# Recurrence stage: the second normalisation and the feed-forward part move one slot back

## The reference

```python
xa = _ln(x, ln1_w, ln1_b)
sx = shifted(xa) - xa
xxx = tanh((xa + sx * maa_x) @ maa_w1).reshape(b, l, 5, DM) ... @ maa_w2
xk, xw, xv, xr, xg = xa + sx * (maa_stack + xxx)
w = exp(-exp(time_decay + tanh(xw @ td_w1) @ td_w2))
r, k, v, g = xr @ Wr.T, xk @ Wk.T, xv @ Wv.T, silu(xg @ Wg.T)
# over the tokens, per head: out = r (u k v + s);  s = k v + w s
og = group_norm(out) * gn_w + gn_b
x1 = x + og * g @ Wo.T
xc = _ln(x1, ln2_w, ln2_b)
sx2 = shifted(xc) - xc
rr = sigmoid((xc + sx2 * ffn_maa_r) @ Wfr.T)
kk = square(relu((xc + sx2 * ffn_maa_k) @ Wfk.T))
return x1 + rr * (kk @ Wfv.T)
```

## Time and profile before

| | us |
|---|---|
| median of 3 runs | 2136.84 (2136.43 to 2137.71) |
| profiled execution | 2138.01, its span 2136.3 |
| TensorE busy | 1944.2 (91% of the span) |
| VectorE busy | 1261.8 (59%) |
| ScalarE busy | 1085.0 (51%) |
| GpSimd busy | 516.4 (24%) |

### The profile page before, as it was taken

One profiled execution on the slowest core, in us unless ns is written; L12 is line 12 of the kernel. 1 busy time (PEld: TensorE's weight loads), 2 busy tenths in 40 slices (PEclk: granted clock), 3 DMA queues, 4 the chain that ended last, 5 costly groups with the idle time before them and its releaser, 6 DMA issues. The chain is left out here.

```text
span 2136.3 us, 40585 instructions
## 1 busy us (share of the span) xinstructions
PE 1944.2 (91%) x15496; PEld 1692.5 (79%) x15496; DVE 1261.8 (59%) x2546; ACT 1085.0 (51%) x2920; POOL 516.4 (24%) x346
## 2 busy tenths in 40 slices
PE   6999996999999999999899999999988986898974
PEld 4677764997999999999699999999978984566653
DVE  6888886235645555555465555555552364888883
ACT  3787877545443344443453344334446543566653
POOL 3555453544200000000240000000005514324220
PEclk9999998999999999999999999999998997899986
DMA  5000001300000000002200000000020000000000
GB/s 188 2 2 2 2 2 42 117 1 6 6 6 5 0 5 5 5 5 90 74 6 1 5 5 5 5 0 5 29 89 1 1 1 1 1 11 6 6 11 10
DMA packets 29534, 40.72 MB, mean 19 GB/s; under 512 B 1923, under 2 KB 21477, under 8 KB 29157
## 3 DMA queue, kind: packets, MB, share of 16 engines
q1 hardware_dynamic: 29412, 39.06, 5.4%
HBM read 32.76 MB, written 2.10 MB: 16 GB/s over the span
## 5 line engine op out<-in xcount | busy, mean ns | idle before, releaser
L761 DVE TENSOR_TENSOR w_head_lo<-banks,w_head_hi 128x512 fp32r<-128x512 f32 x128 | 88.1, 691 | 249.5 <-ACT w_head_hi L673 241.9
L692 ACT ACTIVATE arena<-banks 128x512 f32<-128x512 f32 x128 | 74.9, 597 | 295.1 <-PE banks L551 291.0
L727 DVE TENSOR_TENSOR arena<-banks,cols 128x512 f32<-128x512 f32 x128 | 88.6, 692 | 227.0 <-PE banks L118 226.8
L470 POOL TENSOR_TENSOR w_hT_lo<-arena,w_hT_hi 128x512 fp32r<-128x512 f32 x16 | 20.9, 1306 | 821.0 <-ACT w_hT_hi L647 821.0
L685 ACT ACTIVATE arena<-banks,arena 128x129 f32<-128x129 f32 x512 | 181.3, 376 | 39.5 <-DVE arena L741 39.5
L964 POOL TENSOR_TENSOR arena<-arena 128x1024 f32<-128x1024 f32 x64 | 150.4, 2373 | 162.2 <-DVE arena L1250 162.2
L673 ACT ACTIVATE w_head_hi<-banks 128x512 fp32r<-128x512 f32 x128 | 76.5, 598 | 196.1 <-PE banks L561 196.0
L1168 ACT ACTIVATE arena<-arena 128x128 f32<-128x128 f32 x512 | 163.5, 397 | 1.8 <-DVE arena L1259 1.6
L116 PE MATMUL banks<-w_wo_lo,w_head_hi 128*128 128x256 f32 x512 | 148.6, 290 | 1.3 <-DVE w_head_lo L761 1.3
L116 PE MATMUL banks<-w_hT_lo,w_hi 128*128 128x256 f32 x512 | 146.6, 286 | 0.0
L116 PE MATMUL banks<-w_kv_lo,w_hi 128*128 128x256 f32 x512 | 145.2, 284 | 0.2
(11 more groups left out here) (299 smaller groups left out, 5702.9 us busy)
## 6 DMA issues: line engine op xcount, KB each, us to landing
arena<-in_L_xattn_wq SPq DMA_DIRECT2D x8, 512.0 KB, 4.9
arena<-in_L_xattn_wk SPq DMA_DIRECT2D x8, 512.0 KB, 6.0
arena<-in_L_xattn_wv SPq DMA_DIRECT2D x8, 512.0 KB, 6.9
arena<-in_L_xattn_wo SPq DMA_DIRECT2D x8, 512.0 KB, 9.5
arena<-ctx_t SPq DMA_DIRECT2D x16, 256.0 KB, 2.5
x<-in_x SPq DMA_DIRECT2D x4, 512.0 KB, 6.6
ctx_t<-in_ctx_t SPq DMA_DIRECT2D x1, 2048.0 KB, 11.7
arena<-in_L_xattn_w SPq DMA_DIRECT2D x2, 1024.0 KB, 12.8
```

Source lines behind the costliest of these rows:

```text
L692: act.activation(probT[:, b, :, :], bank[5 + b][:, :].rearrange("p (h q) -> p h q", h=HG), ACT.Copy).then_inc(probT_ok, 1)
L727: dve.tensor_tensor(qT[:, h:h + 2, :], bank[use % 2][:, :].rearrange("p (h t) -> p h t", h=2), core.col(bias, g * HG + h, 2)[:, :, None].t ...
L761: dve.tensor_tensor(head_lo[:, two, :], bank[5 + half][:, :].rearrange("p (h t) -> p h t", h=2), head_hi[:, two, :], ALU.subtract).then_in ...
```

## The change

The part c is cut in two. In slot p it keeps, for pair p-1, the group norm, the product with the gate, `project_out`, `residual` and `row_rstd`; all behind that (`row_shift`, `normalise2`, `copy_xc`, `shift_c`, kk, rr, ff, `gate_ff`, `finish`) is done for pair p-2, called d. One slot is added at the end. On TensorE `project_out` moves behind `project_r`, `a_transpose` and `a_low` move ahead, and the first two mixes of the next pair move to the end of the slot, ahead of `centre`; X and Y are swapped in the mix. On VectorE `residual` moves from between units 1 and 2 to behind `scan` of unit 3, and `shift_a` ahead of unit 3. On ScalarE `normalise2` follows the squares, and `row_rstd` and `tanh_low` come near the end of the slot. On GpSimd the five adds of the mix come in one run ahead of the product with the gate. Slot 8, the first without a unit, has an order of its own. No instruction is added or taken away but for semaphore waits; the two products (gate, r k) stay on GpSimd.

```diff
-        MIX = [X, Y, Z, X, Y]
+        MIX = [Y, X, Z, Y, X]
...
-            for p in range(-1, NP + 1):
+            for p in range(-1, NP + 2):
...
             def slot(p):
-                u, a, c = exists(p), exists(p + 1), exists(p - 1)
-                if a:
-                    add_xa(p + 1, range(0, FR))
-                if c:
+                if exists(p + 1):
+                    add_xa(p + 1, range(0, F))
+                if exists(p - 1):
                     times_gate(p - 1)
-                if a:
-                    add_xa(p + 1, range(FR, F))
+                if exists(p + 1):
                     multiply_rk(p + 1)
-                if c:
-                    finish(p - 1)
+                if exists(p - 2):
+                    finish(p - 2)
...
-                wait(pe, read["xc"], a - 2)
+                wait(pe, read["xc"], a - 3)
...
-            def a_mix(a):
+            def a_mix(a, fs):
                 pe.wait_ge(read["low"], a + 1)
-                for f in range(F):
-                    if f == 0:
+                for f in fs:
+                    if f == 1:
                         wait(pe, read["c"], a)
...
             def project_out(c):
                 pe.wait_ge(z_ok, c + 1)
                 pe.wait_ge(read["td"], min(c + 3, NP))
+                if c == NP - 1:
+                    pe.wait_ge(read["kk"], c)
                 token_major(Z, zT, w["Wo"]).then_inc(ready["out"], 1)
 
             def c_transpose(c):
                 pe.wait_ge(xn2_ok, c * PAIR + PAIR)
-                pe.wait_ge(read["r"], min(c + 3, NP))
+                pe.wait_ge(read["r"], min(c + 4, NP))
                 wait(pe, read["xc"], c)
                 transposes(Y, xn2).then_inc(ready["xc"], 1)
 
             def project_kk(c):
                 pe.wait_ge(xk_ok, c * (2 * KC) + KC)
-                pe.wait_ge(read["out"], c + 1)
+                if c == NP - 2:
+                    pe.wait_ge(read["var"], NP)
+                else:
+                    pe.wait_ge(read["out"], min(c + 2, NP))
+                if c == NP - 1:
+                    pe.wait_ge(read["ff"], c)
                 feature_major(Z, w["Wfk"], xk2).then_inc(ready["kk"], 1)
 
             def project_rr(c):
                 pe.wait_ge(xk_ok, c * (2 * KC) + 2 * KC)
-                pe.wait_ge(read["g"], min(c + 3, NP))
-                pe.wait_ge(read["c"], min(c + 2, NP))
+                pe.wait_ge(read["g"], min(c + 4, NP))
+                pe.wait_ge(read["c"], min(c + 3, NP))
+                wait(pe, read["rr"], c)
                 token_major(X, xr2, w["Wfr"]).then_inc(ready["rr"], 1)
 
             def project_ff(c):
                 pe.wait_ge(read["kk"], c + 1)
+                if c == NP - 2:
+                    pe.wait_ge(read["out"], NP)
                 token_major(Z, kkT, w["Wfv"]).then_inc(ready["ff"], 1)
 
             def slot(p):
-                u, a, c = exists(p), exists(p + 1), exists(p - 1)
+                u, a, c, d = exists(p), exists(p + 1), exists(p - 1), exists(p - 2)
                 if a:
-                    a_mix(p + 1)
+                    if p + 1 == 0:
+                        a_mix(0, (0, 1))
+                    a_mix(p + 1, range(2, F))
                     if p + 1 == 0:
                         core.wait_loaded(pe, stage, "td_w1", "td_w2", "Wk", "Wv", "Wr", "Wg")
                     low_rate(p + 1)
                     project_k(p + 1)
                     project_v(p + 1)
-                if c:
-                    project_out(p - 1)
+                if p == NP:
+                    c_transpose(p - 2)
+                    project_kk(p - 2)
                 if u:
                     sum_heads(p, 0)
                     spread_v(p, 1)
                 if a:
                     project_rate(p + 1)
                     project_r(p + 1)
+                if c:
+                    project_out(p - 1)
                 if u:
                     sum_heads(p, 1)
                 if a:
                     project_g(p + 1)
-                if c:
-                    c_transpose(p - 1)
+                if d and p != NP:
+                    c_transpose(p - 2)
+                if exists(p + 2):
+                    a_transpose(p + 2)
                 if u:
                     sum_heads(p, 2)
-                if c:
-                    project_kk(p - 1)
-                    project_rr(p - 1)
-                if exists(p + 2):
-                    a_transpose(p + 2)
-                if c:
-                    project_ff(p - 1)
-                if u:
-                    sum_heads(p, 3)
+                if d:
+                    if p != NP:
+                        project_kk(p - 2)
+                    project_rr(p - 2)
                 if a:
                     if p + 1 == 0:
                         pe.wait_ge(made, 31)
                     spread_v(p + 1, 0)
+                if d:
+                    project_ff(p - 2)
+                if exists(p + 2):
+                    a_low(p + 2)
+                if a:
                     bonus_sums(p + 1)
                 if u:
+                    sum_heads(p, 3)
+                if exists(p + 2):
+                    a_mix(p + 2, (0, 1))
+                if u:
                     centre(p)
-                if exists(p + 2):
-                    a_low(p + 2)
-                if u:
                     variance(p)
 
...
             def slot(p):
-                u, a, c = exists(p), exists(p + 1), exists(p - 1)
+                u, a, c, d = exists(p), exists(p + 1), exists(p - 1), exists(p - 2)
                 if c:
                     square_centred(p - 1)
-                if a:
-                    tanh_low(p + 1)
+                if d:
+                    normalise2(p - 2)
                 if c:
                     group_rstd(p - 1)
+                if d and p == NP:
+                    copy_xc(p - 2)
                 if u:
                     make_decay(p, 2)
                 if a:
                     tanh_td(p + 1)
+                    copy_k(p + 1)
+                    copy_v(p + 1)
                 if c:
                     scale_rows(p - 1)
-                if a:
-                    copy_k(p + 1)
-                    copy_v(p + 1)
                 if u:
                     make_decay(p, 3)
-                if c:
-                    row_rstd(p - 1)
                 if a:
                     make_rate(p + 1)
                     copy_r(p + 1)
-                if c:
-                    normalise2(p - 1)
+                if exists(p + 2):
+                    normalise(p + 2)
                 if a:
                     tanh_g(p + 1)
-                if c:
-                    copy_xc(p - 1)
+                if d and p != NP:
+                    copy_xc(p - 2)
                 if a:
                     make_decay(p + 1, 0)
                 if exists(p + 2):
-                    normalise(p + 2)
+                    copy_xa(p + 2)
+                if d:
+                    square_relu(p - 2)
+                    sigmoid_rr(p - 2)
                 if c:
-                    square_relu(p - 1)
-                    sigmoid_rr(p - 1)
+                    row_rstd(p - 1)
                 if exists(p + 2):
-                    copy_xa(p + 2)
+                    tanh_low(p + 2)
                 if u:
                     copy_raw(p)
                 if a:
...
+            tanh_low(0)
...
             def slot(p):
-                u, a, c = exists(p), exists(p + 1), exists(p - 1)
+                u, a, c, d = exists(p), exists(p + 1), exists(p - 1), exists(p - 2)
+                if d:
+                    row_shift(p - 2)
                 if u:
                     weigh_keys(p, 0)
                     make_bonus(p)
@@ -2440,29 +2460,34 @@
                     times_r(p, 0)
                 if a:
                     mix(p + 1)
+                if d and p == NP:
+                    shift_c(p - 2)
+                if u:
+                    weigh_keys(p, 1)
+                    scan(p, 1)
                 if c:
                     unit_variance(p - 1)
                 if u:
-                    unit(p, 1)
-                if c:
-                    residual(p - 1)
-                if u:
+                    times_r(p, 1)
                     weigh_keys(p, 2)
                     scan(p, 2)
-                if c:
-                    row_shift(p - 1)
                 if u:
                     times_r(p, 2)
                 if a:
                     make_gate(p + 1)
-                if c:
-                    shift_c(p - 1)
-                if u:
-                    unit(p, 3)
+                if d and p != NP:
+                    shift_c(p - 2)
                 if exists(p + 2):
                     shift_a(p + 2)
+                if u:
+                    weigh_keys(p, 3)
+                    scan(p, 3)
                 if c:
-                    gate_ff(p - 1)
+                    residual(p - 1)
+                if u:
```

(14 more changed lines are left out.)

## The result

The changed kernel takes 2196.6 us (median of four runs, 2195.8 to 2197.8) against 2137.3 before: the ratio is 1.0281, with a 95% interval of 1.0269 to 1.0293. It is slower by 59 us, and 2197 was forecast. The kernel before was measured again beside each group of experiments, at 2135.2 to 2136.9 us; so a difference of less than 2 us between two experiments says nothing.

What follows compares the result with a forecast made beforehand. Queue order, not a full engine, was taken to bound the kernel. 37.05+192.2+47.15+42.5 = 318.9 us against 259.5, plus 0.7, made 60.1 more: 2198.1 profiled, median 2197, range 2160 to 2222.

Steps and rivals of the forecast that it cites:

- The landmarks: Sum from 1873.35 us: 37.05 to slot 2's kk, 192.2 for four slots, 47.15 to centre(7), 42.5 to the end.
- The four slots: From the kk of slot 2 to that of slot 6: 4 x 48.05 = 192.2 us.
- The wait for Z: TensorE's project_kk(p-2) waits until residual(p-1) has read bank Z: 7 us a slot in place of 2.1.
- Steps (a) to (h): One full slot from project_kk to the next, step by step at full clock: 44.05 us against 37.6.
- the ring: Chain through f1, normalise2, f2, g and scan back to kk; 38.7 us a slot if Z is free early.
- The clock: Slow TensorE stretches: 2.6 us behind each kk wait and 1.4 in step (e), k and v; slot 48.05 us.
- The walk: The full slot timed from project_kk to the next, rows' durations added at full clock: 44.05 us.
- Slot 7: No new pair: kk(5) at 31.3, centre(7) at 40.15; 47.15 us with two 2.6 and one 1.8 of clock.
- The tail: centre(7) to the end: 31.8 us before, plus 10.6 (normalise2 1.1, copy_xc and shift_c 3.7, project_out 1.4, row_rstd 4.4).
- Rival 1: Bank Z comes free early enough, only the other order counts: 38.7 us a slot, about 2146; chance 0.11.
- Rival 2: Faster: TensorE's four waits go and VectorE becomes the bound, 34.6 us a slot, about 2125; chance 0.08.
- Rival 3: Slow stretches of TensorE twice as long: slot 51.2 us, about 2217; chance 0.06.

Runs made afterwards that it cites:

- the kk wait filled: Changed kernel plus twelve unused products of weights alone on TensorE ahead of project_kk in slots 2 to 7: 2181.1 us.
- the early residual: Changed kernel with residual of pair p-1 moved on VectorE behind times_r of unit 2, ahead of make_gate and the shift of p-2: 2152.6 us.
- the early residual and the late normalise2: Changed kernel with residual of p-1 ahead of the shift of p-2 and normalise2 behind group_rstd on ScalarE: 2141.2 us.
- The other order of the last slots: Changed kernel with row_rstd ahead of square_relu and, in slots 8 and 9, the last pair's unit_variance, project_out and row_rstd first: 2185.2 us.
- the best kernel here without padding, with five moves: Changed kernel with residual early, normalise2 late, unit_variance behind the mix, row_rstd early, new last two slots, f0 and f1 ahead of centre: 2127.2 us.

## Why the prediction was right

**The landmarks.** The first late kk was forecast for 1911.1 us (1873.35 + 0.7 + 37.05) and came at 1911.49. The four slots behind it took 191.7 us (192.2 forecast), from there to centre of the last pair 46.1 (47.15), and the tail 42.4 (42.5). No part is off by more than about 1 us. Inside the parts, though, terms were off by up to 2 us and made up for each other: that 2197 came so near to 2196.6 is in part luck, and what the runs bear out is the wait and the shape of the slot.

**The four slots.** They took 49.84, 47.83, 47.81 and 46.26 us, where each was to take 48.05. The first kept a longer slow stretch (its mean clock is 0.77): rr behind kk took 3.03 us in place of 2.02, and the mix f2 2.10 in place of 1.15. The last is 1.55 us shorter than the one ahead of it, since slot 6 has no `shift_a` ahead of the add: there is no pair 8. The sum overlooked that, and the first slot made up for it.

**The wait for Z.** Forecast 7 us in place of 2.1, measured 6.8, and its end is the add of `residual`. The move of `residual` alone gave back 44 us: shown.

**Steps (a) to (h).** At full clock they gave 44.05 us; with the kk wait filled the slot measured 44.58. VectorE's wait at f2 was 2.9 us (2.5 forecast). That the gate product has slack was shown by doubling it; that normalise2 is on the ring, by the pair of kernels with the early residual.

**The clock.** Here a term was too large, and steps walked too short made up for it. The slot at full clock with the early residual and the late normalise2 is the measure: there f0 starts 10.13 us behind kk, and the first sum over heads 24.99, which is 26.0 with the 1.0 us of normalise2. In the changed kernel they start 11.97 and 29.11 us behind kk. So behind the kk wait 1.8 us were lost, and not 2.6. In k and v 1.3 were lost, near the 1.4 taken: the pair is 2.2 us longer than at full clock, but 1.0 of that lies where the sum waited for unit_variance anyhow. Together 3.1 us against the 4.0 taken; the slot with the kk wait filled, 44.58 against 47.83, says 3.3. The walk was short by what is missing: it has the first sum over heads at 24.85 and not 26.0 (f2 already at 16.8 and not 17.5), and from there to the next kk 19.2 us, where 18.7 were measured.

**Slot 7.** It was to take 35.7 us up to kk(5) with its clock terms and took 35.63, though project_out there took 2.90 us and not the 3.8 of the sum; the way on to centre(7) took 10.50 and not 11.45, which is 1.65 us above the walk at full clock, where 2.6 were taken.

**The tail.** Its loss was forecast as 10.6 us and measured as 10.6, but by luck. First the changed kernel, then the kernel before:

```profile
2149.36 2.03 PE L2066 MATMUL banks<-arena 128*128 128x512 f32 x2 [2.66 <-ACT arena L2240]
...
2153.07 0.60 ACT L2245 ACTIVATE arena<-banks 128x512 f32<-128x512 f32 x1 [3.77 <-PE banks L2067]
...
2170.20 0.69 DVE L2412 TENSOR_TENSOR x<-x,banks 128x512 f32<-128x512 f32 x1 [7.57 <-PE banks L1989]
...
2174.49 0.29 ACT L2263 ACTIVATE arena<-mean_var_new,eps 128x2 f32<-128x2 f32 x1
```

```profile
2103.05 0.60 ACT L2229 ACTIVATE arena<-banks 128x512 f32<-128x512 f32 x1 [2.07 <-PE banks L2069]
...
2114.65 0.69 DVE L2394 TENSOR_TENSOR x<-x,banks 128x512 f32<-128x512 f32 x1 [6.34 <-PE banks L1991]
...
2116.45 0.30 ACT L2247 ACTIVATE arena<-mean_var_new,eps 128x2 f32<-128x2 f32 x1 [5.71 <-DVE mean_var_new L2402]
```

From the last add of `residual` to the logarithm of row_rstd were 4.29 us in place of 1.80: row_rstd cost 2.5 us, and the sum had 4.4 for it. In its place stand two losses of clock that the sum left out: from centre to the square 3.71 us in place of 2.03, and 0.9 us in the last rr and ff, which took 4.54 in place of 3.66. The other terms were about right: normalise2 1.0 (1.1 forecast), copy_xc and shift_c 3.3 (3.7), project_out's wait for Z 1.4 (1.4). The other order of the last slots gave 7.2 us of the 10.6 back; 1.7 of these are the clock at centre, so some 5.5 us of the loss lie in the order.

**The rivals.** Rival 1 (about 2146 us, the kk wait not binding) is in effect what the early residual made: 2152.6 us, 6 above its price. Its slots took 39.2 to 41.1 us at a clock of 0.88 to 0.91, where the price was 38.7 at full clock. It didn't happen in the changed kernel, as the wait is binding. Rival 2 gave 2125 us for an order that is rid of the waits; the best kernel here without padding, with five moves, reached 2127. Rival 3 asked for a slot of 51.2 us with nearly twice the slow stretches, which didn't come. The drain that the Trainium skill adds to a table load (ScalarE: Activation LUTs, What ACT_TABLE_LOAD costs) is not there in the changed kernel either (timeline of ScalarE):

```profile
1979.79 0.69 ACT L2249 ACTIVATE arena<-banks,eps 128x512 f32<-128x512 f32 x1
1980.49 1.28 ACT L2252 ACT_TABLE_LOAD   x1
```

The load begins 0.01 us after the logarithm has ended, and takes 1.28 us as in the earlier trace rows; the forecast rightly went by the row.

## What to carry to other kernels

When an operation is moved one slot back on one engine, list for each bank the writers and readers in the order of the new slot: the write of the older work may now have to wait for a read of the newer one, and it is the place of that reader on its own engine that counts. A move of a single instruction group, `residual`, decided over 44 of the 59 us. A wait on TensorE is to be priced with the products behind it at half clock, here 1.8 us for a wait of 6.8. And when a sum of many terms comes out right, each term is still to be read from the trace: here row_rstd was 1.9 us too dear and the clock of a slot 0.9, and other errors hid both.

## What the runs showed of the hardware

A slow stretch moves with small shifts of the work, and can swallow a gain. With normalise2 late, 1.0 us was saved ahead of the logarithm, and in three slots rr behind kk grew from 2.0 to 3.1 us. In one kernel slots alternated between 36.1 and 38.9 us with the same instructions, and in another all of them held 35.84 us. One kk ran at half clock behind a wait of 0.35 us (3.68 us), while others behind the same wait took 1.99. So where TensorE waits several times a slot, a difference of 1 to 3 us a slot between two orders may be clock alone, and the granted clock is to be read beside it.
